# Level codes in bf16, an issue order split over two engines, and double-buffered projection parts in a one-layer language-model tower

## The reference, cut to what matters

```python
lvl = clip(lvl + is_open(tok) - is_close(tok), 0, 31)      # a scan over each sequence, gives levels
h = level_emb[levels] * 0.15                               # only 32 different rows
h = h + attention_with_relative_positions(layernorm(h))    # 16 heads, softmax((AC + BD) / 4)
x = layernorm(h)
q, k, v = (rmsnorm(x) * norm1_w) @ (wq, wk, wv)            # second attention
x2 = x + softmax(q @ k.T / 4) @ v @ wo
h = h + x2 + shared_ffn(rmsnorm(x2)) + top2_of_8_experts(rmsnorm(x2))
```

## Time and profile before

| | us |
|---|---|
| median of 3 runs | 947.49 (946.36 to 947.91) |
| the profiled execution | 950.77 |
| its span, first to last instruction | 949.0 |
| `tables`, to the first matmul of `level_attention` | 0 to 53.5 |
| `level_attention` | 53.5 to 284.1 |
| `project` | 284.1 to 393.8 |
| `full_attention` | 393.8 to 533.9 |
| `route` | 533.9 to 597.8 |
| `experts` | 597.8 to 949.0 |

### The profile page before, as it was taken

How to read it: one execution, slowest core, us unless ns; L and a number is a source line. 1 busy time by engine, 2 the same in 40 slices (tenths; PEclk the granted TensorE clock), 3 DMA queues, 4 the chain that set the end, 5 groups by cost and what they waited for, 6 DMA issues and landing times. The chain is left out here.

```text
span 949.0 us, 19708 instructions
## 1 busy us (share of the span) xinstructions
PE 842.3 (89%) x7404; PEld 560.6 (59%) x7405; DVE 477.6 (50%) x1097; ACT 333.8 (35%) x563; POOL 148.5 (16%) x155
## 2 busy tenths in 40 slices
PE   5989999999988949699999877999989999999994
PEld 3346666666666838466666666455646556565552
DVE  7356655655645625266667487361133334433432
ACT  1357666666642414355555222211011111111110
POOL 4000000000001314200000022027202222222221
PEclk7579999999987979799999888799999999999998
DMA  5200000000001692256955200682312222222221
GB/s 205 77 2 2 2 2 2 3 2 2 3 2 40 119 130 83 67 68 90 106 70 66 85 0 0 250 328 102 122 46 45 45 44 40 39 44 45 45 36 20
DMA packets 68488, 58.80 MB, mean 62 GB/s; under 512 B 5504, under 2 KB 60104, under 8 KB 68432
## 3 DMA queue, kind: packets, MB, share of 16 engines
q1 hardware_dynamic: 60512, 47.60, 22.2%
q0 software_dynamic: 7152, 9.38, 5.9%
q10 hardware_dynamic: 768, 1.02, 0.3%
HBM read 35.02 MB, written 22.95 MB: 61 GB/s over the span
## 5 line engine op out<-in xcount | busy, mean ns | idle before, releaser
L1100 DVE TENSOR_REDUCE fa_m<-ps 128x2 bf16<-128x512 f32 x128 | 81.8, 685 | 35.4 <-PE ps L998 34.7
L1349 POOL DMA_INDIRECT out<-ex_Y,ex_to x39 | 60.6, 1553 | 207.7 <-DVE ex_Y L1592 204.8
L1080 ACT ACTIVATE fa_PT<-ps 128x1024 f32<-128x1024 f32 x64 | 65.6, 1024 | 67.9 <-PE ps L1016 67.9
L1417 PE MATMUL ps<-ex_WG,ex_xT 128*128 x156 | 78.5, 627 | 5.0 <-ACT ex_xT L1470 0.6
L595 ACT ACTIVATE la_PT<-ps 128x512 f32<-128x512 f32 x128 | 69.5, 594 | 33.1 <-PE ps L501 33.1
L1572 DVE TENSOR_TENSOR ex_hd<-ps,ex_sl 128x512 f32<-128x512 f32 x39 | 27.0, 692 | 101.9 <-PE ps L1417 101.9
L1430 PE MATMUL ps<-ex_WD,ex_hT 128*128 x312 | 73.8, 379 | 0.9 <-DVE ex_hT L1576 0.9
L1430 PEld LDWEIGHTS ps<-ex_WD,ex_hT 128*128 128x128 f32 x312 | 59.2, 190 | 25.3 <-issue 19.3
L1417 PE MATMUL ps<-ex_WU,ex_xT 128*128 x156 | 73.3, 592 | 0.0
L628 DVE TENSOR_REDUCE la_m<-ps 128x4 bf16<-128x512 bf16 x64 | 44.3, 692 | 47.8 <-PE ps L494 46.8
L609 DVE CAST V<-ps 96x512 bf16<-96x512 f32 x64 | 43.9, 686 | 36.8 <-PE ps L466 36.8
(11 more groups left out here) (259 smaller groups left out, 1494.4 us busy)
## 6 DMA issues: line engine op xcount, KB each, us to landing
QK<-qk_parts SPq DMA_DIRECT2D x96, 128.0 KB, 5.9
qk_parts<-pj_parts SPq DMA_DIRECT2D x16, 384.0 KB, 2.8
expert_in<-SG SPq DMA_DIRECT2D x1, 5070.0 KB, 14.8
ex_XR<-expert_in SPq DMA_DIRECT2D x39, 130.0 KB, 2.1
ex_WG<-in_e_gate SPq DMA_DIRECT2D x8, 512.0 KB, 9.8
ex_WU<-in_e_up SPq DMA_DIRECT2D x8, 512.0 KB, 9.6
ex_WD<-in_e_down SPq DMA_DIRECT2D x8, 512.0 KB, 9.7
out<-HS SPq DMA_DIRECT2D x4, 512.0 KB, 3.7
```

Source lines behind the costliest of these rows:

```text
L1080: nc.scalar.activation(PT[:, grp % 2, k:k + 2], ps[:, 2 + 2 * (hp % 2):4 + 2 * (hp % 2)].rearrange("p k (j i) -> p k j i", j=2), ACT.Exp, ...
L1100: nc.vector.reduce_max(m[:, par, h], ps[:, h % 2].rearrange("p (f j) -> p f j", f=2), AX.X).then_inc(s_max, 1)
L1349: nc.gpsimd.indirect_dma_start(out=outs, out_offset=bass.IndirectOffsetOnAxis(ap=to[:, n:n + 1], axis=0), in_=Y[:, n], in_offset=None, com ...
L1417: last = mm(ps[:, bk + n], xT[:, n, cc], w[:, bass.ds(e + cc * F, F)], start=cc == 0, stop=cc == 1)
```

## The change

In `tables`: `lev` and `lev4` become bf16, and ScalarE copies `sel` into a bf16 `selB`, so the broadcasts are bf16 matmuls. Tokens are loaded second and have a semaphore of their own; constants count on another (`const`), which `lev4` and ScalarE wait for. The sixteen one-hot tiles are divided 6 (VectorE) and 10 (ScalarE), each side through its two banks. TensorE, VectorE and ScalarE get a new order: the first two codes for ScalarE come right behind `lev4`, before the levels broadcasts, which now use two banks in turn.

In `project`: `parts` has two buffers, and `high(t)` waits for the store of trip t-2. `rest(t)` waits for `low(t-1)`, since `r1` remains single. SP's order is store(t) and, from t = 2, four of the 24 loads. The loops of SP, POOL, ACT and DVE are written out; PE's remains.

```diff
-        acc, Dl, nD, rD, zer, lev = (sb(n, [B, S], F32) for n in ("acc", "Dl", "nD", "rD", "zer", "lev"))
+        lev, selB = sb("lev", [B, S], BF16), sb("selB", [B, B, P], BF16)
-        h4, lev4, iotaL = sb("h4", [B, HG], F32), sb("lev4", [B, S, HG], F32), sb("iotaL", [P, L], F32)
+        h4, lev4, iotaL = sb("h4", [B, HG], F32), sb("lev4", [B, S, HG], BF16), sb("iotaL", [P, L], F32)
+        CUT = 6
+        OWN = (range(0, CUT), range(CUT, TILES))
                 sp.dma_start(emb[:], a["emb"]).then_inc(s_in[1], 16)
+                sp.dma_start(tok[:], a["x"]).then_inc(s_in[0], 16)
                 sp.dma_start(g.identF[:], a["ident"]).then_inc(s_in[4], 16)
-                sp.dma_start(tok[:], a["x"]).then_inc(s_in[0], 16)
@@ scalar
+                act.wait_ge(s_in[8], 80)
+                copy(selB[:], sel[:]).then_inc(s_selb, 1)
+                for x in range(4):
+                    one_hot(x)
+                act.wait_ge(s_erT, 1)
+                copy(g.ErT[:], ps[0:KP, 4].bitcast(BF16)[:, 0:512]).then_inc(s_act, 1)
+                one_hot(4)
                 act.wait_ge(s_qkT, 1)
                 for n in range(2):
                     copy(qkT[:, n]...)
+                for x in range(5, len(OWN[1])):
+                    one_hot(x)
@@ vector
-                dve.wait_ge(s_in[0], 96)
+                dve.wait_ge(s_in[0], 16)
...
+                for x in range(2):
+                    one_hot(x)
                 dve.wait_ge(s_ac, 1)
...
+                for x in range(2, len(OWN[0])):
+                    one_hot(x)
@@ tensor, behind the projections
+                pe.wait_ge(s_selb, 1)
+                pe.wait_ge(s_lv, 2)
+                for x in range(2):
+                    codes(1, x)
+                for q in range(2):
+                    levels(q)
+                for x in range(2, 4):
+                    codes(1, x)
                 ... (transposes of Er)
+                codes(1, 4)
                 ... (waits for VT; transposes of Q and K)
+                codes(1, 5)
+                for q in range(2, 4):
+                    levels(q)
+                for x in range(2):
+                    codes(0, x)
                 ... (the 16 products of L389, the transpose of lev)
+                for x in range(2, CUT):
+                    codes(1, x + 4)
+                    codes(0, x)
@@ project
-        parts = sb("parts", [P, 2, 3, DC * GC], BF16)
+        parts = sb("parts", [P, 2, 2, 3, DC * GC], BF16)
-                for t in range(2):
-                    store(t)
-                sp.wait_ge(s_moved, 64 + 2 * 32)
-                for b in range(2):
-                    load_packed(g, sp, b, b)
-                with sp.Fori(2, GN) as t:
-                    store(t)
-                sp.wait_ge(s_moved, 64 + GN * 32)
+                for t in range(GN):
+                    store(t)
+                    if t >= 2:
+                        b, part = divmod(t - 2, 3)
+                        sp.wait_ge(s_st[b], 32)
+                        load_packed(g, sp, b, b, range(2 * part, 2 * part + 2))
+                for r in range(2):
+                    sp.wait_ge(s_st[r], GN // 2 * 32)
 def high(i, n):
-                    act.wait_ge(s_moved, i * 32 + 64)
+                    if i >= 2:
+                        act.wait_ge(s_st[i % 2], i // 2 * 32)
 def rest(i, n):
+                    if i:
+                        dve.wait_ge(s_lo[n], i)
-                with act.Fori(0, GN - 2) as t:
+                for t in range(GN - 2):
```

More of the change, by code:

```diff
@@ L158, in tables @@
     sem, ps = g.sem, g.ps
[L159 removed]
+    s_in = [sem("in_" + n) for n in ("tok", "tab", "w", "er", "id", "wo", "bias", "dump", "const")]
     s_ohb, s_ohx = ([sem("tab_" + n + k) for k in names(2)] for n in ("codes", "onehot"))
     s_dve, s_act, s_pool = sem("tab_dve"), sem("tab_act"), sem("tab_pool")
[L162 to L163 removed]
+    s_lv, s_lvp, s_oh, s_lvt, s_sq, s_ln, s_xt, s_xtc, s_proj, s_sp, s_qkT, s_qkTc, s_ac, s_er, s_erT, s_idb, s_rs, s_zero, s_selb = (
+        sem("tab_" + n) for n in "levels levelsB onehot3 levelsT square norm xT xTc proj split qkT qkTc ac er erT idb rstd zero selB".split())
     with ExitStack() as c:
@@ L222, in _ @@
                     copy(qkT[:, n].rearrange("p h l -> p (h l)"), ps[0:KP, 5 + n].bitcast(BF16)[:, 0:512]).then_inc(s_qkTc, 1)
[L223 to L232, removed]
+                for x in range(5, len(OWN[1])):
+                    one_hot(x)
                 act.wait_ge(s_act, 1)
-                act.wait_ge(s_ohx[1], B)
+                act.wait_ge(s_ohx[1], len(OWN[1]))
             @block.gpsimd
@@ L352, in _, with levels @@
                 last.then_inc(s_proj, 1)
-                pe.wait_ge(s_lv, 1)
[L355 to L358, removed]
+                def levels(q):
+                    if q >= 2:
+                        pe.wait_ge(s_oh, q - 1)
+                    for b in (2 * q, 2 * q + 1):
+                        last = mm(ps[0:L3, q % 2, (b % 2) * S:(b % 2 + 1) * S], selB[:, b, 0:L3], lev[:], start=True, stop=True)
+                    last.then_inc(s_lvp, 1)
                 def codes(k, x):
@@ L714, in project @@
     s_q, s_hi, s_r1, s_mi, s_lo = ([sem("pj_" + n + k) for k in "qk"] for n in ("made_", "high_", "rest_", "mid_", "low_"))
+    s_st = [sem("pj_stored" + n) for n in names(2)]
     with ExitStack() as c:
@@ L760, in low @@
                     pool.wait_ge(s_mi[n], i + 1)
-                    nc.gpsimd.tensor_tensor(parts[:, n, 2], r1[:, n], parts[:, n, 1], ALU.subtract).then_inc(s_lo[n], 1)
+                    nc.gpsimd.tensor_tensor(parts[:, i % 2, n, 2], r1[:, n], parts[:, i % 2, n, 1], ALU.subtract).then_inc(s_lo[n], 1)
                 powers(0)
-                with pool.Fori(0, GN - 1) as t:
+                for t in range(GN - 1):
                     powers(t + 1)
@@ L947, in trip @@
                     rest(t, 1)
-                with dve.Fori(0, GN - 3) as t:
-                    do.enter(t, 2 + 2 * GT)
+                for t in range(GN - 3):
                     trip(t, True, True)
-                do.leave(GN - 3)
                 trip(GN - 3, True, False)
```

67 lines of the change are left out of this document (32 added, 35 removed).

## The result

The changed kernel takes 911.96 us (median of 4 runs, 910.60 to 915.19), the kernel before 947.70 beside it (4 runs, 946.36 to 949.35). The ratio is 0.9623 with an interval of 0.9604 to 0.9643: 36 us faster. The forecast was 909.5, in a range of 904 to 917. The profiled execution took 913.05 us, its span is 911.2; 912.8 and 911.0 were forecast.

A forecast was written before the change was run, and what follows sets the result against it. Bounds: TensorE's float32 codes in `tables`; TensorE in `project`, plus stalls from stores queued behind 24 loads. Gains 22.2 + 15.8 = 38.0 us from the median 947.49 give 909.5 us, range 904 to 917.

The forecast's parts named there:

- The walk through three queues: `tables`: following TensorE, ScalarE and VectorE in order, both sides end about 31.0 us against 53.19, a gain of 22.2.
- only work ahead of the token chain reads it; I take zero: `tables`: moving the identity matrix's load behind the tokens costs one issue, 0.7 us at most, taken as zero.
- the tie of the two queues: `tables`: ScalarE's seventh code queues on TensorE behind VectorE's first two and the sixteen products, so is ready at 25.0 us.
- rival 3: `tables`: bf16 codes bring little, TensorE staying at 1.78 us a tile; gain 9 instead of 22, 922.5 us; chance 0.04.
- rival 1: Only sizes differ: ScalarE and VectorE in lock-step in `tables`, clock a little later; +4 us, 913.5; chance 0.17.
- the stall: `project`: with no loads ahead of store 2, trip 3 to 4 returns from 22.92 to 9.56 us, gaining 13.36.
- the last two waits: `project`: ScalarE's last two waits for stores (25.0 less 18.9 us) overlap matmuls needed anyway; given 0.2 us.
- zero, at worst 0.5: `project`'s end: four loads issued behind the last store, 1.6 to 2.8 us, against 2.7 for its landing; cost zero, at worst 0.5.
- Rivals 2 and 4: For rival 2 see its line; rival 4: DMA contention in `project` at its extreme makes the kernel slower, 972 us; chance 0.02.
- rival 2: `project`: mixed loads and stores are slower than apart, a trip needing 12 us; 12 us lost, 921.5; chance 0.06.
- no interval above 10.6: `project`: sign of being right, that eight first transposes of TensorE have no interval above 10.6 us.
- The clock between blocks: Entry of `level_attention`: clock rise may come sooner or up to 4 us later; -1 to +2 us, taken as zero.

The follow-up runs named there:

- tokens_late: The changed kernel with the token chain waiting for all constants again; 935.01 us in one run, on another chip where the kernel before took 970.72.
- written_out: The kernel before with the loops of SP, POOL, ACT and DVE in `project` written out, nothing else; 948.49 us in one execution.
- tables_only: The changed `tables` with `project` of the kernel before; 924.20 us against 946.79 for the kernel before, ratio 0.9774.
- loads_ahead: The changed kernel with its two buffers, but all 24 loads in one piece behind the second store, as before; 917.48 us, ratio 0.9683.
- one_buffer: The changed kernel with `parts` single again, `high(t)` waiting for the store of trip t-1; 912.01 us, ratio 0.9631.
- project_only: The changed `project` with `tables` of the kernel before; 933.15 us, ratio 0.9850 to the kernel before.
- eight_each: The changed kernel with eight one-hot tiles for each engine instead of 6 and 10; 910.96 us in one execution.
- warm_entry: The changed kernel with unused identity products on TensorE where it idled before `project`'s first transposes; 932.76 us on another chip, ratio 0.9618 to the kernel before.
- after_again: The changed kernel, unchanged, measured again on another chip; 936.47 us, ratio 0.9640 to the kernel before.
- f32_new_order: The changed kernel with `lev`, `lev4` and `selB` in float32; 931.19 us, ratio 0.9823 to the kernel before.

## Why the prediction was right, point by point

**`tables`: 22.2 forecast, 21.9 measured (53.5 to 31.57).** The walk through three queues held nearly place by place, and its errors cancelled.
- The token cast starts at 5.90, not 5.65. The step "only work ahead of the token chain reads it; I take zero" was wrong: the cast of the identity matrix (L290) is ahead of the token chain in VectorE's own queue and waited 1.14 us for the moved load. In eight other profiles of the new order it waited 0.27 to 0.68 (1.11 in tokens_late), and the token cast stands at 5.33 to 5.60. The six of them with bf16 codes and the cut at six have `tables` at 30.8 to 31.1 us, so 21.9 is a low value of what the change gives and 22.4 to 22.7 the usual one.
- The `sel` copy at 1.06 us ended near 8.6, covered, as forecast.
- The first Square starts at 13.38 (13.15 forecast). ScalarE's pitch for a tile is 1.33 us (14.73 to 16.06), not 687 + 721 ns: a Square starts before the record of the Relu ahead of it has ended.
- `VT` ended at 20.33 (20.5), with the dearer copies counted; the seventh Square started at 25.40 (25.0) behind a 1.49 wait, as the tie of the two queues said. Before the tenth, where 0.3 was forecast, ScalarE stood 0.10.
- Both sides end at 31.04 and 30.78 (30.9 and 30.7). The first matmul is at 31.57 and not at 31.3, also because it stands 0.53 behind ScalarE's end; the 0.33 of before, which the forecast carried over, is that behind VectorE's.
- A code costs 0.61 us (0.63 taken), which is the end of rival 3, and the lock-step of rival 1 isn't there.

**`project`: 15.8 forecast, 14.8 measured (109.7 to 94.9).** Term by term:
- the stall: 22.92 to 9.45 gives 13.47 (13.36 forecast); the clock behind it: 11.82 to 9.45 gives 2.37 (2.26). The 0.11 more in each is the written-out loop, which written_out shows with nothing else changed; it was forecast zero, and over five intervals it is 0.55.
- the last two waits: zero instead of 0.2. The intervals 8.58 and 6.62 follow 8.69 and 6.62.
- the lead-in and first trip: 0.91 lost (16.18 + 10.85 against 15.56 + 10.56 = 26.12). No step of the forecast had this place, though the earlier trace rows has a 7 over it. It is the clock at the entry, early or late with the same code; with the same entry in both, nothing would be lost here.
- the tail: 14.91 against 14.44, so 0.47 lost. The forecast took "zero, at worst 0.5", with SP's issue of the four loads as what might outlast the store's landing. The size was at its worst end, and the mechanism is another one. Before, tables_only, written_out and loads_ahead, without loads behind the last store, have tails of 14.44, 14.44, 14.32 and 14.36 us; one_buffer, project_only, eight_each and warm_entry, with them, 14.92, 14.94, 14.93 and 14.94. So the loads cost 0.5. But in after their issue ends at 353.29 + 2.64 = 355.93, and the last store, issued at 352.85, lands only at 356.44, 0.47 ahead of the next block; in all fourteen profiles that block starts 0.41 to 0.47 behind this landing. What the loads do is slow it. The landing of the last store in after, then in loads_ahead:

```profile
qk_parts<-pj_parts SPq DMA_DIRECT2D x1, 384.0 KB, 3.6
```

```profile
qk_parts<-pj_parts SPq DMA_DIRECT2D x1, 384.0 KB, 3.0
```

It is 3.6 us in all eight profiles with loads behind it and 3.0 to 3.1 in the six without.

The sum is 13.47 + 2.37 + 0.33 (three more intervals at 0.11) - 0.91 - 0.47 = 14.8. Rivals 2 and 4 fell: with loads and stores mixed, 128 GB/s on the mean of 300 to 345 us, a store landed in 3.3 us, and TensorE's trip didn't grow. The 0.6 us by which loads slow the last store is all that is left of rival 2. The agreement within 1 us has luck in it: `project` with the new order is 92.2 to 95.2 us long over the profiles, by its entry, and with the old one 105.4 to 110.3.

**Signs of being wrong.** No wait of `high` on a DMA, no store's landing above 3.7 us (10 was the sign), no gap of VectorE for codes late in `tables`, and `level_attention` at 230.5 against 230.6. One sign failed: "no interval above 10.6" met 10.85, for the clock at the entry. The block length of 93.9 became 94.9.

**The clock between blocks: zero forecast, within -1 to +2.** In after the products of `level_attention` are at the lower clock until 36.04 us, and the next ones, at 36.81, are not: the rise comes 4.5 to 5.2 us behind the block's start, where before had 3.5. In after_again, the same kernel, these next products still take as long as at the lower clock:

```profile
36.81 0.38 PE L507 MATMUL ps<-XS,OH 96*128 96x128 bf16 x4 [0.78 <-ACT XS L596]
```

```profile
36.11 0.59 PE L507 MATMUL ps<-XS,OH 96*128 96x128 bf16 x4 [0.77 <-ACT XS L596]
```

There the rise comes at about 39.7, 8.8 us behind the start, and the block is 231.2 us long instead of 230.5. So even a rise 3.6 us or more later goes with only 0.7 us on the block, inside the bounds.

**The total.** 38.0 us were forecast, and 37.8 lie between the spans (949.0 to 911.2), which looks better than it is: 1.4 of it is `route` (63.9 to 62.5), where the change does nothing. `route` is 61.6 to 64.2 us long in the profiles with and without the change alike. Between the medians lie 35.7 us, with 33.8 to 37.5 by the interval of the ratio, so 38.0 was slightly too much. `tables` gave 0.3 less than forecast and `project` 1.0 less, and the other blocks gave 1.1 unforeseen, which makes 37.8. The rest is an assumption of the sum, that all of the profiled execution's distance over the median would remain after the change: it was 3.07 us over the median of the four runs of before and is 1.09 over that of after, so 2.0 less. Where these 3.07 lay can't be told from one profile. The time still came within 2.5 us of the forecast, inside the range and inside the likeliest case's own bounds of 905 to 914.

## What to carry to other kernels

On an in-order DMA queue, look at what stands ahead of each store whose buffer is wanted again: moving the bulk loads behind the stores gave all of the gain, and a second buffer none on top of it. Where two changes meet on one path, work them out together: the new order, with its early tokens and its cut, was worth 2.8 us while TensorE was full with float32 codes and 5.8 us once they were bf16. For each moved load, look for its first reader in every engine's queue. And keep bulk loads from behind the last store of a block: here they made it land in 3.6 us instead of 3.0, and the barrier waits for that landing.

## What was not expected of the hardware

**The granted clock in the records can be wrong for most of a block.** The same stretch of after and then of after_again, which is the same kernel, from the first codes into `level_attention` (columns as in the earlier trace rows):

```profile
12.60:36.00 23.40, 16.53 (x64) 6.11 (x64) 19.37 (x42) 17.22 (x27) 6.02 (x15) 1.00 0.57 223
```

```profile
12.60:36.00 23.40, 15.93 (x63) 5.77 (x61) 19.07 (x40) 17.83 (x28) 5.81 (x14) 0.50 0.57 223
```

The one says 1.00 (2.4 GHz) and the other 0.50 (1.2 GHz), yet a code takes 0.60 us in both (610 and 598 ns on the mean), and from the start of `VT` to the block's end both take 11.66 us. The durations side with 0.50: the products of 512 columns start 0.42 us apart in after (31.57 and 31.99 in the timeline above), and 0.22 apart at 40.56 and 40.78. 512 columns in 0.42 us are 1.2 a nanosecond, the lower of the two levels. The product at 54.80 in the earlier trace rows has the same 0.63 us, and there the record stood at 0.50. f32_new_order has 1.00 in its window above and codes of 1074 ns, as long as those of the earlier trace rows. So the durations of a known instruction decide, and the 9s of after's page in `tables` aren't a gain. The Trainium skill, "TensorE: Matmul & The Clock Gate", Part 1, "Seeing it yourself", calls these trace events "observed to be unreliable"; this trace agrees.

**Busy isn't the same as fast.** TensorE was busy 12.40 of 13.50 us with 8-row float32 codes in before and its clock remained at 0.50. f32_new_order was busy 36.95 of 38.00 us, and its codes took no less.

**The same code of a block meets different clocks.** The start of `project` costs 24.3 us to the second transpose (tables_only, 14.81 + 9.50) or 27.0 (after), with TensorE idle about 2.4 us ahead of the first one in both. What goes with it is how late the clock rises behind the block's start, 7.0 us or 9.8, before any difference in what TensorE did. What sets that is open. Whether one kernel can have either is open too: the only kernel with two profiles, after and after_again, had the slow entry both times (16.18 + 10.85 and 16.20 + 10.86), but its rise in `level_attention` came 4.5 to 5.2 us behind the start in the one and 8.8 in the other.

**One block was 24 us longer on one chip.** `experts` took 375 to 376 us there and 350 to 352 elsewhere, with the same code, and no other block was longer there. The place can be told. In after_again ScalarE stood still here for 33.80 us, where one_buffer has a wait of 9.74 for TensorE:

```profile
639.24 1.09 ACT L1491 ACTIVATE ex_sil<-ps 128x512 f32<-128x512 f32 x2 [33.80 <-remote]
```

All four profiles of that chip have this wait, with the same 33.8 us, and one of VectorE of 23.8 to 30.2 us beside it; "remote" says that no instruction of the profile released them. TensorE then waited for both, some 20 us in all. The cause is open.
